# Latent attention in steps of four heads instead of two, in a four-layer mixer kernel on one core

## The chip, the cores and the metric

The kernel runs on one core of one Trainium2 chip. The metric is device time in microseconds of one execution of the whole program; lower is better. The core has TensorE (PE) for matrix products and transpositions, VectorE (DVE) and ScalarE (ACT) for element-wise work and reductions, GpSimd (POOL) and DMA queues. PE reads SBUF and writes only to PSUM, which the kernel uses as eight banks of 128 x 512 fp32. DVE and ACT take results out of PSUM.

## The reference

The program is four layers of `x = x + attention(norm(x)) * silu(ffn(norm(x)))` over 8192 tokens of width 128 (32 sequences of 256 tokens). Only the attention of layer 0 is touched by the change:

```python
# D_MODEL, N_HEADS, N_KV, HEAD_DIM, D_LAT = 128, 8, 2, 128, 32;  N_REP = 4
q = (x @ wq).reshape(Bq, Tq, N_KV, N_REP, HEAD_DIM)
k_lat = (x @ wk_down).reshape(Bq, Tq, N_KV, D_LAT)
v_lat = (x @ wv_down).reshape(Bq, Tq, N_KV, D_LAT)
k = jnp.einsum('bkhl,ld->bkhd', k_lat, wk_up)
v = jnp.einsum('bkhl,ld->bkhd', v_lat, wv_up)
scores = jnp.einsum('bqhrd,bkhd->bhrqk', q, k) * scale
scores = jnp.where(causal, scores, jnp.finfo(scores.dtype).min)
probs = jax.nn.softmax(scores, axis=-1)
y = jnp.einsum('bhrqk,bkhd->bqhrd', probs, v)
return y.reshape(Bq, Tq, N_HEADS * HEAD_DIM) @ wo
```

The up-projections are folded into `wq` and `wo` beforehand, so keys, queries and values have 32 elements per head, and four heads fill the 128 partitions.

## The kernel before

`first_layer` runs: the norm, the routing of tokens to experts, `latent_attention` for sequences 0 to 15, the expert FFN, `latent_attention` for sequences 16 to 31, and the gate. The later layers follow and are the same before and after. So the changed function runs twice (a run is called a half below), each time over `pairs` = 8 pairs of sequences (index `i`; `u` is the sequence of the pair). Each engine has its own program, written out in full; engines meet only through counting semaphores (`STEPS`), where `S["exps"].at(i, j)` is the value reached when step `j` of pair `i` is done. An engine runs its list in order, so a wait holds up everything behind it.

A sequence has 8 heads, in two groups `c` of four (one key/value head each). Before, a **step** `j` is two heads, four steps to a sequence. Of one step:

- PE, `pe_scores` (L699 to L706): for each of the two heads a 128 x 256 and a 128 x 128 block of scores (the causal blocks only) from 32 partitions, into one bank a head; then masks added by four 64 x 64 bf16 products (L706). Steps alternate between banks 0-1 and 2-3, so the scores of `j` wait for the exponentials of `j - 2`.
- DVE, `rowmax` (L876, L877): the negated row maxima, out of the two banks.
- ACT, `exps` (L838): four exponentials with row sums.
- PE, `pe_turn` (L715): six 128 x 128 transpositions of the probabilities into banks 4 and 5; DVE copies both banks at once to SBUF (L898, 128 x 768).

Every second step, `pe_mix` (L727) multiplies four heads' transposed probabilities with the values into bank 6. Once a sequence: key, query and value projections (L743, L743, L754), the spread of the inverse row sums (`pe_spread`, L737), the product of the two on DVE (`ot`, L891) and the output projection (L749), all through bank 7. ACT copies queries, spread sums, values and outputs (L854, L850, L861, L865), DVE copies keys (L902). POOL widens the inverse sums (L803), copies the input (L809), and issues four indirect DMAs a sequence (L518 scatter, L526 gather) that have to do with the experts.

The order of the work around the change is that of the bodies of `body(i)`: in turn `t`, PE does scores `t + 1`, transpositions `t - 1`, the value product every second turn, and one of the once-a-sequence products.

Of the kernel before, what the change touches and what calls it, by code (L numbers as in the profile page):

```python
# [27 lines left out]
P = 128  # L28
# [42 lines left out]
class Stage:  # L71
# [21 lines left out]
    "projected", "freed_act", "freed_dve", "scores", "masked", "rowmax", "exps", "turned", "turned_sb",  # L93
# [576 lines left out]
def latent_attention(nc, ps, m, w, first_pair, pairs, move, weights):  # L670
# [4 lines left out]
    with ExitStack() as mem:  # L675
# [5 lines left out]
        pr, nm, pt = buf("probs", P, 2, 2, W), buf("minus_max", P, 2, 2, 2), buf("probs_t", P, 4, 2, W)  # L681
# [7 lines left out]
        def pe_scores(pe, i, j):  # L689

            u, c, s = j % 8 // 4, j % 4 // 2, j % 2
            pe.wait_ge(*S["exps"].at(i, j - 2))
            if j % 4 == 0:
                pe.wait_ge(*S["k_sb"].at(i, j // 4))
                pe.wait_ge(*S["q_sb"].at(i, j // 4))
            b0 = 2 * s
            for e in range(2):
                rows = slice(32 * (2 * s + e), 32 * (2 * s + e) + 32)
                pe.matmul(ps[:, b0 + e, P:W], qt[rows, u, c, P:T], kt[rows, u, c, :], start=True, stop=False)  # L699
            for e in range(2):  # L700
                rows = slice(32 * (2 * s + e), 32 * (2 * s + e) + 32)
                pe.matmul(ps[:, b0 + e, 0:P], qt[rows, u, c, 0:P], kt[rows, u, c, 0:P], start=False, stop=False)
            for e in range(2):
                rows = slice(64 * e, 64 * e + 64)
                for h in range(2):
                    mm = pe.matmul(bank(ps, b0 + e, 3, P)[64 * h:64 * h + 64, ::2], one[rows, rows],  # L706
                                   hide[rows, h:h + 1].to_broadcast([64, 2, P]), start=False, stop=True)
            mm.then_inc(*S["scores"].inc)

        def pe_turn(pe, i, j):  # L710
            pe.wait_ge(*S["exps"].at(i, j))
            pe.wait_ge(*S["turned_sb"].at(i, j - 1))
            for e in range(2):
                for k in range(3):
                    mm = pe.transpose(ps[:, 4 + e, k * P:(k + 1) * P], pr[:, j % 2, e, k * P:(k + 1) * P], m["ident"][:])  # L715
            mm.then_inc(*S["turned"].inc)

        def pe_mix(pe, i, g):

            u, c = g % 4 // 2, g % 2  # L720
            pe.wait_ge(*S["turned_sb"].at(i, 2 * g + 1))
            pe.wait_ge(*S["v_sb"].at(i, g // 2))
            if c == 0:
                pe.wait_ge(*S["attended"].at(i, g // 2 - 1))
            for kb in range(2):
                for r in range(4):
                    mm = pe.matmul(ps[32 * r:32 * r + 32, 6, c * T + kb * P:(c + 1) * T], v[:, u, kb, c * LAT:(c + 1) * LAT],  # L727
                                   pt[:, (2 * g + r // 2) % 4, r % 2, kb * T:T + kb * P], start=(kb == 0), stop=(kb == 1))
            mm.then_inc(*S["mixed"].inc)

        def pe_spread(pe, i, n):
            pe.wait_ge(*S["widened"].at(i, n))
            if here(i, n + 2, 2):
                pe.wait_ge(*S["k_sb"].at(i, n + 2))
# [23 lines left out]
        names = dict(copied=2, scores=8, rowmax=8, exps=8, turned=8, turned_sb=8, mixed=4, rowsum=2, widened=2, spread=2,  # L758
                     spread_sb=2, attended=2, q_ps=2, q_sb=2, k_ps=2, k_sb=2, v_ps=2, v_sb=2, o_ps=2, o_sb=2)
        with Stage(pairs, **names), Stage(1, moved0=TOK), nc.Block() as block:  # L760
            @block.tensor
            def _(pe):
                def body(i):
                    for t in range(8):
                        u, at = t // 4, t % 4
                        if here(i, t + 1, 8):
                            pe_scores(pe, i, t + 1)
                        if here(i, t - 1, 8):
                            pe_turn(pe, i, t - 1)
                        if t % 2 and here(i, (t - 3) // 2, 4):  # L770
                            pe_mix(pe, i, (t - 3) // 2)
                        if at == 0 and here(i, u - 1, 2):
                            pe_spread(pe, i, u - 1)
                        if at == 1 and here(i, u + 1, 2):
                            pe.wait_ge(*S["k_sb"].at(i, u + 1))
                            pe.wait_ge(*S["spread_sb"].at(i, u - 1))
                            pe_project(pe, i, u + 1, lambda c: wq[:, c], "q_ps")
                        if at == 2:
                            if here(i, u + 1, 2):
                                pe.wait_ge(*S["q_sb"].at(i, u + 1))  # L780
                            if here(i, u - 1, 2):
                                pe_out(pe, i, u - 1)
                            if here(i, u + 1, 2):
                                pe_v(pe, i, u + 1)
                        if at == 3 and here(i, u + 2, 2):
                            pe.wait_ge(*S["o_sb"].at(i, u - 1))
                            pe.wait_ge(*S["v_sb"].at(i, u + 1))
                            pe.wait_ge(*S["copied"].at(i, u + 2))
                            pe_project(pe, i, u + 2, lambda c: wk[:, c].rearrange("p r l -> p (r l)"), "k_ps")

                written_out(pairs, 1, 1, body)
# [33 lines left out]
            def _(act):  # L825
                act.preload_act_table_set("exp_and_others")

                def exps(i, j):
                    u, c, s = j % 8 // 4, j % 4 // 2, j % 2
                    act.wait_ge(*S["rowmax"].at(i, j))  # L830
                    act.wait_ge(*S["turned"].at(i, j - 2))
                    if j % 4 == 0:
                        act.wait_ge(*S["rowsum"].at(i, j // 4 - 2))
                    for e in range(2):
                        head = 4 * c + 2 * s + e
                        for qb in range(2):
                            span = slice(qb * P, P + qb * T)
                            last = act.activation(pr[:, j % 2, e, span], ps[:, 2 * s + e, span], ACT.Exp,  # L838
                                                  bias=nm[:, s, qb, e:e + 1], accum_out=sums[:, u, qb, head:head + 1])
                    last.then_inc(*S["exps"].inc)  # L840

                def body(i):
                    for t in range(8):
                        u, at = t // 4, t % 4
                        if here(i, t, 8):
                            exps(i, t)
                        if at == 0 and here(i, u - 1, 2):
                            act.wait_ge(*S["spread"].at(i, u - 1))
                            act.wait_ge(*S["attended"].at(i, u - 2))
                            act.activation(rt[:], ps[:, 7], ACT.Copy).then_inc(*S["spread_sb"].inc)  # L850
                        if at == 1 and here(i, u + 1, 2):
                            act.wait_ge(*S["q_ps"].at(i, u + 1))
                            act.wait_ge(*S["scores"].at(i, 4 * u - 1))
                            act.activation(qt[:, 1 - u], bank(ps, 7, 2, T), ACT.Copy).then_inc(*S["q_sb"].inc)  # L854
                        if at == 2:
                            if here(i, u - 1, 2):
                                act.wait_ge(*S["o_ps"].at(i, u - 1))
                            if here(i, u + 1, 2):
                                act.wait_ge(*S["v_ps"].at(i, u + 1))
                                act.wait_ge(*S["mixed"].at(i, 2 * u - 1))  # L860
                                act.activation(v[:, 1 - u], ps[:, 7, T:T + P].rearrange("p (t l) -> p t l", t=2),  # L861
                                               ACT.Copy).then_inc(*S["v_sb"].inc)
                            if here(i, u - 1, 2):
                                act.wait_ge(S["first"].sem, PRIME)
                                act.activation(m["s"][:, bass.ds((i * 2 + 2 * first_pair + u - 1) * T, T)], ps[:, 7, 0:T], ACT.Copy)\  # L865
                                    .then_inc(*S["o_sb"].inc)

                written_out(pairs, 1, 1, body)

            @block.vector  # L870
            def _(dve):
                def rowmax(i, j):
                    s = j % 2
                    dve.wait_ge(*S["scores"].at(i, j))
                    dve.wait_ge(*S["exps"].at(i, j - 2))
# [1673 lines left out]
```

## Time and profile before

| | us |
|---|---|
| three runs: median (lowest, highest) | 2933.48 (2930.82, 2941.59) |
| the profiled execution: its own time | 2933.75 |
| span of its trace | 2932.0 |
| PE busy | 2690.3 (92%) |
| DVE busy | 2159.2 (74%) |
| ACT busy | 1948.2 (66%) |
| POOL busy | 1060.5 (36%) |
| mean granted clock of TensorE | 0.956 |

The span holds many stages with different limits, so shares over the span say little of this change. In a timeline row the first number is the start from the start of the span, the second the time from the first start to the last end of the merged instructions, then engine, line, operation, tiles and shapes; a bracket at the end gives the idle time before it and who ended it. A matmul on fp32 shows as two records, a transposition as one. Ends of matmuls are modelled, so the distance from one start to the next start of the same engine is the better measure of what a piece of work takes on PE; the second number is what the engines that wait for it see.

### The profile page before, as it was taken

To read this page: it belongs to the slowest core of one execution; us is meant where nothing else is said; L and a number is where in the kernel's file an instruction comes from. 1 tells how busy PE (TensorE), PEld (TensorE's weight loads), DVE (VectorE), ACT (ScalarE), POOL (GpSimd) and SP (SyncE) were. 2 spreads that over 40 slices of the span, in tenths; PEclk is the share of its full clock that TensorE was granted. 3 is DMA by queue.
4 is the path that set the end of the run, shared out by engine and by line. 5 is a ranking of instruction groups with operands and counts; after the bars stand their busy time and mean duration, and the time that the engine had idled before them with its cause. 6 is when DMAs were issued, how large, how long until landed. Compare 5 with 4: busy or idle time off the path is not lost. (4 is left out here: it accounts for less than half of the span.)

```text
span 2932.0 us, 62151 instructions
## 1 busy us (share of the span) xinstructions
PE 2690.3 (92%) x21644; PEld 1794.8 (61%) x21644; DVE 2159.2 (74%) x3742; ACT 1948.2 (66%) x5578; POOL 1060.5 (36%) x1228
## 2 busy tenths in 40 slices
PE   7799899997889879978879999999898999999898
PEld 4577797774554444445537777777444777777644
DVE  4576565776674569956769999998446999999766
ACT  4366565666763464435359999998446999999744
POOL 0233343331000254410035555564214655555431
PEclk9799998998999979979989999999998999999999
DMA  4200121000000000022000000000000000000000
GB/s 145 76 22 21 47 73 29 20 23 12 9 17 0 1 1 0 0 61 31 9 20 2 2 2 2 2 2 2 20 1 9 2 2 2 2 2 2 2 22 36
DMA packets 83170, 53.93 MB, mean 18 GB/s; under 512 B 28848, under 2 KB 75568, under 8 KB 82864
## 3 DMA queue, kind: packets, MB, share of 16 engines
q1 hardware_dynamic: 78768, 41.56, 5.1%
q0 software_dynamic: 4096, 8.40, 1.0%
q8 instruction: 179, 2.93, 0.4%
q14 instruction: 127, 1.04, 0.1%
HBM read 31.59 MB, written 18.35 MB: 17 GB/s over the span
## 5 line engine op out<-in xcount | busy, mean ns | idle before, releaser
L2149 ACT ACTIVATE probs<-banks,minus_max,rnorm 128x128 f32<-128x128 f32 x1024 | 460.0, 469 | 4.2 <-DVE minus_max L2245 2.8
L2021 PE MATMUL banks<-weights,hf 128*128 128x512 f32 x768 | 429.6, 643 | 24.5 <-POOL hf L462 13.5
L2064 POOL TENSOR_TENSOR qk_cross<-qk_raw,rope_scaled 128x512 f32<-128x512 f32 x256 | 325.5, 1272 | 25.4 <-ACT qk_raw L2182 11.5
L2074 POOL TENSOR_TENSOR qk_rot<-qk_rot,rnorm 128x512 f32<-128x512 f32 x128 | 133.5, 1043 | 291.3 <-DVE qk_rot L2278 282.9
L2149 ACT ACTIVATION_READ_ACCUMULATOR probs<-banks,minus_max,rnorm 128x1 f32 x1024 | 222.6, 217 | 0.0
L838 ACT ACTIVATE probs<-banks,minus_max 128x128 f32<-128x128 f32 (+1 forms) x512 | 207.9, 425 | 13.2 <-DVE minus_max L877 11.8
L2225 DVE COPY probs_t<-banks 128x512 f32<-128x512 f32 x256 | 175.8, 687 | 53.7 <-PE banks L1999 53.5
L1999 PEld LDWEIGHTS banks<-ident,probs 128*128 128x128 f32 x1024 | 126.9, 141 | 134.4 <-issue 134.4
L2271 DVE TENSOR_TENSOR qk_rot<-qk_raw,rope_scaled 128x512 f32<-128x512 f32 x256 | 175.5, 726 | 0.0
L2259 DVE TENSOR_REDUCE sumsq<-qk_sq 128x16 f32<-128x1024 f32 x128 | 154.8, 1209 | 26.9 <-issue 19.9
L2030 PE MATMUL banks<-ident,qk_rot 128*128 128x128 f32 x1024 | 159.7, 279 | 10.2 <-DVE qk_rot L2278 5.0
L2278 DVE TENSOR_TENSOR qk_rot<-qk_rot,qk_cross 128x1024 f32<-128x1024 f32 x128 | 161.5, 1261 | 4.4
L2241 DVE TENSOR_REDUCE minus_raw<-banks 128x8 f32<-128x1024 f32 x128 | 155.5, 1215 | 7.0 <-PE banks L1991 7.0
L1999 PE MATMUL banks<-ident,probs 128*128 128x128 f32 x1024 | 153.9, 273 | 6.0 <-DVE probs_t L2225 5.8
L2021 PEld LDWEIGHTS banks<-weights,hf 128*128 128x128 f32 x768 | 117.4, 192 | 53.0 <-POOL hf L462 15.1
L2013 PE MATMUL banks<-v_tok,probs_t 128*64 128x64 f32 x3072 | 148.4, 226 | 0.0
L2464 DVE SCALAR_TENSOR_TENSOR qk_rot<-banks,b1t,qk_rot 128x512 f32<-128x512 f32 x96 | 71.9, 750 | 103.3 <-ACT qk_rot L2417 89.1
L441 POOL TENSOR_SCALAR ln_rows<-ln_rows,ln_moments,ln_scale 128x128 f32<-128x128 f32 x64 | 49.8, 792 | 254.4 <-ACT ln_scale L423 254.4
L2030 PEld LDWEIGHTS banks<-ident,qk_rot 128*128 128x128 f32 x1024 | 114.7, 142 | 41.8 <-issue 38.6
L2013 PEld LDWEIGHTS banks<-v_tok,probs_t 128*64 128x64 f32 x3072 | 130.6, 138 | 11.9 <-issue 10.0
L2115 PE MATMUL banks<-ot,weights 128*128 128x128 f32 x1024 | 136.3, 276 | 0.0
L2163 ACT ACTIVATE qk_sq<-qk_raw 128x1024 f32<-128x1024 f32 x128 | 134.2, 1048 | 0.1
(356 smaller groups left out, 6976.2 us busy)
## 6 DMA issues: line engine op xcount, KB each, us to landing
sorted_x<-zero_rows SPq DMA_DIRECT2D x10, 512.0 KB
rows_in<-sorted_x SPq DMA_DIRECT2D x18, 256.0 KB, 3.1
sorted_y<-rows_out SPq DMA_DIRECT2D x18, 256.0 KB, 2.4
x_res<-in_x SPq DMA_DIRECT2D x8, 512.0 KB, 7.1
out_x<-x_res SPq DMA_DIRECT2D x16, 256.0 KB, 2.0
w1b<-in_L_ffn_w SPq DMA_DIRECT2D x8, 256.0 KB
s_branch<-in_L_ffn_w SPq DMA_DIRECT2D x8, 256.0 KB
w1g<-in_L_ffn_W SPq DMA_DIRECT2D x8, 256.0 KB, 3.0
```

Source lines behind the costliest of these rows:

```text
L838: last = act.activation(pr[:, j % 2, e, span], ps[:, 2 * s + e, span], ACT.Exp, bias=nm[:, s, qb, e:e + 1], accum_out=sums[:, u, qb, head: ...
L1999: mm = pe.transpose(ps[:, 4, n * P:(n + 1) * P], pr[:, k % 2, 4 * h + n], m["ident"][:])
L2013: mm = pe.matmul(ps[64 * w:64 * w + 64, 5, at], pt[:, h, n * P + 64 * w:n * P + 64 * w + 64], vm[:, at] if tb and not w else va[:, k % 4, ...
L2021: pe.matmul(ps[:, misc(k, j)], hf[:, n // 2 % 2, 0, n % 2 * P:(n % 2 + 1) * P], wqkv[:, w:w + QW], start=True, stop=True).then_inc(*S[name ...
L2030: mm = pe.transpose(ps[:, misc(k, j), c * P:(c + 1) * P], st[:, n % 4, first:first + P], m["ident"][:])
L2064: return pool.tensor_tensor(by_half(tw[:, n, at]), by_half(qk[:, n, at])[:, :, ::-1, :], tab[:, n, 2 * w + 1].rearrange("p (a d) -> p a d" ...
L2149: last = act.activation(pr[:, k % 2, head], ps[:, 2 * (k % 2) + par, c * P:(c + 1) * P], ACT.Exp, scale=rn[:, k % 4, head:head + 1], bias= ...
L2225: dve.tensor_copy(pt[:, h], ps[:, 4]).then_inc(*S["turned_sb"].inc)
L2241: dve.tensor_reduce(nr[:].rearrange("p (b c) -> p b c", b=2), ps[:, 2 * (k % 2):2 * (k % 2) + 2].rearrange("p b (c t) -> p b c t", c=4), A ...
L2259: dve.tensor_reduce(ss[:], by_head(sq[:]), AX.X, ALU.add).then_inc(*S["sumsq"].inc)
L2271: last = dve.tensor_tensor(by_head(st[:, n, at]), by_head(qk[:, n % 2, at]), tab[:, n % 2, 2 * w:2 * w + 1].to_broadcast([P, HEADS, DH]), ...
L2278: dve.tensor_tensor(st[:, n], st[:, n], tw[:, n % 2], ALU.add).then_inc(*S["rotated"].inc)
```

## The change

The unit of work becomes the group `g` of four heads, two to a sequence. `pe_scores` fills banks 0 to 3 at once, so there is no second set of banks, and the scores of `g` wait for the exponentials of `g - 1`. All eight mask products stand together; a signal is given after the fourth and after the eighth. The twelve transpositions of a group go in three lots of four, each to one whole bank, 4 or 5 in turn. They are those of the group before, `g - 1`. ACT copies the first lot (`lead_sb`), ahead of its exponentials of `g`, DVE the other two. The value products of `g - 2` stand ahead of the scores of `g`. The copies of keys and those of queries and of spread sums change engines: keys go from DVE to ACT, the other two from ACT to DVE. The key projection is one sequence ahead instead of two.

```diff
-        pr, nm, pt = buf("probs", P, 2, 2, W), buf("minus_max", P, 2, 2, 2), buf("probs_t", P, 4, 2, W)
+        pr, nm, pt = buf("probs", P, 2, 4, W), buf("minus_max", P, 2, 2, 2, 2), buf("probs_t", P, 2, 4, W)
-        def pe_scores(pe, i, j):
-            pe.wait_ge(*S["exps"].at(i, j - 2))
+        def pe_scores(pe, i, g):
+            u, c = g % 4 // 2, g % 2
+            pe.wait_ge(*S["exps"].at(i, g - 1))
+            if c == 0:
+                pe.wait_ge(*S["k_sb"].at(i, g // 2))
+                pe.wait_ge(*S["q_sb"].at(i, g // 2))
+            for r in range(4):
+                rows = slice(32 * r, 32 * r + 32)
+                pe.matmul(ps[:, r, P:W], qt[rows, u, c, P:T], kt[rows, u, c, :], start=True, stop=False)
+            for r in range(4):
+                rows = slice(32 * r, 32 * r + 32)
+                pe.matmul(ps[:, r, 0:P], qt[rows, u, c, 0:P], kt[rows, u, c, 0:P], start=False, stop=False)
+            for s in range(2):
+                for e in range(2):
+                    rows = slice(64 * e, 64 * e + 64)
+                    for h in range(2):
+                        mm = pe.matmul(bank(ps, 2 * s + e, 3, P)[64 * h:64 * h + 64, ::2], one[rows, rows],
+                                       hide[rows, h:h + 1].to_broadcast([64, 2, P]), start=False, stop=True)
+                mm.then_inc(*S["scores"].inc)
+        def pe_turn(pe, i, g, t):
+            if t == 0 and not here(i, g + 1, 4):
+                pe.wait_ge(*S["exps"].at(i, g))
+            if t == 2:
+                pe.wait_ge(*S["lead_sb"].at(i, g))
+            else:
+                pe.wait_ge(*S["turned_sb"].at(i, 2 * (g - 1) + t))
+            for k in range(4):
+                mm = pe.transpose(ps[:, 4 + (g + t) % 2, k * P:(k + 1) * P], blocks(pr, g, t)[:, k * P:(k + 1) * P],
+                                  m["ident"][:])
...
             @block.tensor
             def _(pe):
+                def slot(i, g):
+                    u = g // 2
+                    if here(i, g - 2, 4):
+                        pe_mix(pe, i, g - 2)
+                    if here(i, g, 4):
+                        pe_scores(pe, i, g)
+                    if here(i, g - 1, 4):
+                        pe_turn(pe, i, g - 1, 0)
+                    if g % 2 == 0 and here(i, u - 1, 2):
+                        pe_spread(pe, i, u - 1)
+                    if g % 2 == 1 and here(i, u + 1, 2):
+                        pe.wait_ge(*S["k_sb"].at(i, u + 1))
+                        pe_project(pe, i, u + 1, lambda c: wq[:, c], "q_ps")
+                    if here(i, g - 1, 4):
+                        pe_turn(pe, i, g - 1, 1)
+                        pe_turn(pe, i, g - 1, 2)
+                    if g % 2 == 0 and here(i, u + 1, 2):
...
+                            pe.wait_ge(*S["spread_sb"].at(i, u - 1))
...
+                        pe_project(pe, i, u + 1, lambda c: wk[:, c].rearrange("p r l -> p (r l)"), "k_ps")
+                    if g % 2 == 1:
...
+                            pe.wait_ge(*S["q_sb"].at(i, u + 1))
...
+                            pe_out(pe, i, u - 1)
...
+                            pe_v(pe, i, u + 1)
...
             def _(act):
+                def slot(i, g):
...
+                        act.activation(blocks(pt, g - 1, 0), ps[:, 4 + (g - 1) % 2], ACT.Copy).then_inc(*S["lead_sb"].inc)
+                    if here(i, g, 4):
+                        exps(i, g)
...
             def _(dve):
+                def turned(i, g, t):
+                    dve.wait_ge(*S["turned"].at(i, 3 * g + t))
+                    if t == 1:
+                        dve.wait_ge(*S["mixed"].at(i, g - 2))
+                    dve.tensor_copy(blocks(pt, g, t), ps[:, 4 + (g + t) % 2]).then_inc(*S["turned_sb"].inc)
```

On PE, two of the four steps of a sequence in the steady part before: scores (`kt,qt`), masks (`hide`), six transpositions (`ident,probs`), with the once-a-sequence products between.

```order
244 L699 MATMUL banks<-kt,qt 128x256 x2
245 L702 MATMUL banks<-kt,qt 128x128 x2
246 L706 MATMUL banks<-hide,ident_bf 64x2x128 x4
247 L715 MATMUL banks<-ident,probs 128x128 x6
248 L749 MATMUL banks<-ot,wo_lat 128x256 x2
249 L754 MATMUL banks<-wvd,xf 128x64 x2
250 L699 MATMUL banks<-kt,qt 128x256 x2
251 L702 MATMUL banks<-kt,qt 128x128 x2
252 L706 MATMUL banks<-hide,ident_bf 64x2x128 x4
253 L715 MATMUL banks<-ident,probs 128x128 x6
```

The same engine and place of the changed kernel: one slot (the odd one of a sequence), then the value products that stand ahead of the next scores.

```order
232 L701 MATMUL banks<-kt,qt 128x256 x4
233 L704 MATMUL banks<-kt,qt 128x128 x4
234 L709 MATMUL banks<-hide,ident_bf 64x2x128 x8
235 L721 MATMUL banks<-ident,probs 128x128 x4
236 L752 MATMUL banks<-xf,wq_lat 128x256 x2
237 L721 MATMUL banks<-ident,probs 128x128 x8
238 L758 MATMUL banks<-ot,wo_lat 128x256 x2
239 L763 MATMUL banks<-wvd,xf 128x64 x2
240 L735 MATMUL banks<-probs_t,v_tok 32x256 x4
241 L735 MATMUL banks<-probs_t,v_tok 32x128 x4
```

Four heads' scores and masks now stand in one block instead of two, and only once-a-group work follows until the next block. The count of products and transpositions is as before.

DVE in the steady part, before: maxima and copies of 768 columns alternate, with `kt` and `ot` between.

```order
148 L886 RECIPROCAL inv_sums<-row_sums 128x16
149 L876 TENSOR_REDUCE minus_max<-banks 128x2
150 L877 TENSOR_REDUCE minus_max<-banks 128x2
151 L898 COPY probs_t<-banks 128x768
152 L876 TENSOR_REDUCE minus_max<-banks 128x2
153 L877 TENSOR_REDUCE minus_max<-banks 128x2
154 L898 COPY probs_t<-banks 128x768
155 L891 TENSOR_TENSOR ot<-banks,inv_spread 128x512
```

The same of the changed kernel, one sequence: even slot, then odd slot.

```order
146 L901 RECIPROCAL inv_sums<-row_sums 128x16
147 L886 TENSOR_REDUCE minus_max<-banks 128x2 x4
148 L914 COPY inv_spread<-banks 128x512
149 L894 COPY probs_t<-banks 128x512 x2
150 L906 TENSOR_TENSOR ot<-banks,inv_spread 128x512
151 L886 TENSOR_REDUCE minus_max<-banks 128x2 x4
152 L917 COPY qt<-banks 128x512
153 L894 COPY probs_t<-banks 128x512 x2
```

The copies of the transposed probabilities now come after the copy of spread sums or queries, which come after all four maxima.

## Rows read from the trace of the kernel before

**Rows 1.** The table of windows: window and length, busy us of each engine, clock, DMA.
```profile
95.72:317.81 222.09, 216.23 (x1984) 158.66 (x1984) 145.84 (x240) 133.57 (x577) 77.23 (x96) 0.96 0.14 42
239.56:252.51 12.95, 12.95 (x126) 9.61 (x126) 9.08 (x16) 8.23 (x36) 4.80 (x7) 1.00 0.07 22
102.91:115.26 12.35, 12.35 (x59) 8.65 (x58) 4.72 (x8) 4.95 (x22) 3.94 (x5) 0.50 0.91 242
440.00:467.00 27.00, 23.12 (x202) 22.50 (x200) 12.98 (x28) 14.74 (x23) 9.24 (x22) 1.00 0.18 50
1010.00:1050.00 40.00, 25.33 (x132) 22.51 (x132) 31.09 (x200) 34.48 (x108) 35.31 (x46) 0.74 0.00 1
```

**Rows 2.** The timeline of PE over one sequence of the steady part.
```profile
243.22 0.70 PE L699 MATMUL banks<-kt,qt 32*128 32x256 f32 x4
...
244.07 0.30 PE L706 MATMUL banks<-hide,ident_bf 64*64 64x256 bf16 x4
244.30 0.87 PE L715 MATMUL banks<-ident,probs 128*128 128x128 f32 x6
245.01 1.03 PE L749 MATMUL banks<-ot,wo_lat 128*128 128x256 f32 x4
245.88 0.55 PE L754 MATMUL banks<-wvd,xf 128*128 128x64 f32 x4
246.36 0.70 PE L699 MATMUL banks<-kt,qt 32*128 32x256 f32 x4
...
248.26 0.86 PE L727 MATMUL banks<-probs_t,v_tok 128*32 128x256 f32 x16
249.04 1.13 PE L743 MATMUL banks<-xf,wk_lat 128*128 128x256 f32 x4
250.10 0.70 PE L699 MATMUL banks<-kt,qt 32*128 32x256 f32 x4
...
251.90 0.60 PE L737 MATMUL banks<-ident,inv_wide 128*128 128x128 f32 x4
252.43 0.70 PE L699 MATMUL banks<-kt,qt 32*128 32x256 f32 x4
```

**Rows 3.** The timeline of ACT, same sequence.
```profile
246.96 0.37 ACT L838 ACTIVATE probs<-banks,minus_max 128x128 f32<-128x128 f32 x1
...
247.75 0.38 ACT L838 ACTIVATE probs<-banks,minus_max 128x128 f32<-128x128 f32 x1
...
248.45 0.23 ACT L838 ACTIVATION_READ_ACCUMULATOR probs<-banks,minus_max 128x1 f32 x1
...
252.54 0.60 ACT L850 ACTIVATE inv_spread<-banks 128x512 f32<-128x512 f32 x1 [2.19 <-PE banks L737]
253.03 0.36 ACT L838 ACTIVATE probs<-banks,minus_max 128x128 f32<-128x128 f32 x1
```

**Rows 4.** The timeline of DVE, same sequence.
```profile
243.58 0.69 DVE L891 TENSOR_TENSOR ot<-banks,inv_spread 128x512 f32<-128x512 f32 x1 [1.00 <-PE banks L727]
244.43 0.42 DVE L876 TENSOR_REDUCE minus_max<-banks 128x2 f32<-128x256 f32 x1 [0.16 <-PE banks L706]
244.77 0.68 DVE L877 TENSOR_REDUCE minus_max<-banks 128x2 f32<-128x512 f32 x1
245.37 0.95 DVE L898 COPY probs_t<-banks 128x768 f32<-128x768 f32 x1
...
250.21 0.69 DVE L902 COPY kt<-banks 128x512 f32<-128x512 f32 x1 [0.76 <-PE banks L743]
250.82 0.24 DVE L886 RECIPROCAL inv_sums<-row_sums 128x16 f32<-128x16 f32 x1
```

**Rows 5.** More of the timelines of PE and POOL, one mix earlier.
```profile
241.37 0.86 PE L727 MATMUL banks<-probs_t,v_tok 128*32 128x256 f32 x16
241.82 0.96 POOL L518 DMA_INDIRECT sorted_x<-token_rows,row_of_token  x1 [0.30 <-issue]
```

**Rows 6.** Who waited for whom, 130 to 320 us: total, times, longest.
```profile
DVE ot L891 <- PE banks L727: 13.7, 14, 1.0
```

More of the change, by code:

```diff
@@ L710, in pe_turn, with blocks @@
[L710 to L715, printed above, removed]
+        def blocks(x, g, t):
+            return x[:, g % 2].rearrange("p h w -> p (h w)")[:, 4 * t * P:4 * (t + 1) * P]
+        def pe_scores(pe, i, g):
[17 more added lines that the diff above has]
+                mm.then_inc(*S["scores"].inc)
@@ L793, in _ @@
+                written_out(pairs, 1, 1, lambda i: [slot(i, g) for g in range(4)])
             @block.gpsimd
@@ L826, in _ @@
                 act.preload_act_table_set("exp_and_others")
[L828 to L839, printed above, removed]
-                    last.then_inc(*S["exps"].inc)
@@ L842, in body @@
[L842 to L866, printed above, removed]
@@ L868, in _, with exps @@
-                written_out(pairs, 1, 1, body)
+                def exps(i, g):
+                    u, c = g % 4 // 2, g % 2
+                    act.wait_ge(*S["turned"].at(i, 3 * (g - 2) + 2))
+                    if c == 0:
+                        act.wait_ge(*S["rowsum"].at(i, g // 2 - 2))
+                    for s in range(2):
+                        act.wait_ge(*S["rowmax"].at(i, 2 * g + s))
+                        for e in range(2):
+                            for qb in range(2):
+                                span = slice(qb * P, P + qb * T)
+                                head = 4 * c + 2 * s + e
+                                last = act.activation(pr[:, g % 2, 2 * s + e, span], ps[:, 2 * s + e, span], ACT.Exp,
+                                                      bias=nm[:, g % 2, s, qb, e:e + 1],
+                                                      accum_out=sums[:, u, qb, head:head + 1])
+                    last.then_inc(*S["exps"].inc)
@@ L870, in _ @@
+                written_out(pairs, 1, 1, lambda i: [slot(i, g) for g in range(4)])
             @block.vector
             def _(dve):
[L872 to L875, printed above, removed]
-                    dve.tensor_reduce(nm[:, s, 0], ps[:, 2 * s:2 * s + 2, 0:P], AX.X, ALU.max, negate=True)
-                    dve.tensor_reduce(nm[:, s, 1], ps[:, 2 * s:2 * s + 2, P:W], AX.X, ALU.max, negate=True)\
-                        .then_inc(*S["rowmax"].inc)
@@ L904, in _, with rowmax @@
-                written_out(pairs, 1, 1, body)
+                def rowmax(i, g, s):
+                    dve.wait_ge(*S["scores"].at(i, 2 * g + s))
+                    dve.wait_ge(*S["exps"].at(i, g - 2))
+                    for qb in range(2):
+                        last = dve.tensor_reduce(nm[:, g % 2, s, qb], ps[:, 2 * s:2 * s + 2, qb * P:P + qb * T], AX.X,
+                                                 ALU.max, negate=True)
+                    last.then_inc(*S["rowmax"].inc)
+                def turned(i, g, t):
[3 more added lines that the diff above has]
+                    dve.tensor_copy(blocks(pt, g, t), ps[:, 4 + (g + t) % 2]).then_inc(*S["turned_sb"].inc)
@@ L905, in latent_attention @@
+                written_out(pairs, 1, 1, lambda i: [slot(i, g) for g in range(4)])
         S["loaded"].base += 16 * len(weights)
```

130 lines of the change are left out of this document (57 added, 73 removed).

## The prediction

> **What bounds the kernel now.** I read the windows first, then the timelines of PE, ACT and DVE over one sequence, then the list of waits.
>
> The window table shows the first half from the first input copy to the last output copy: 222.09 us for 16 sequences. In its steady part one sequence takes 12.95 us, and PE is busy for all 12.95 of them, at a granted clock of 1.00, that is 2.4 GHz. DVE is busy 9.08 us and ACT 8.23 us [rows 1]. So PE sets the pace. The second half is the same code with another DMA. 16 x 12.95 = 207.2 us; the other 15 us of a half are the start, where PE stood at half clock (0.50, 1.2 GHz) for 12.35 us [rows 1], and the run-out.
>
> What PE does with a step is in its timeline, read from start to start. Scores of two heads take 244.07 - 243.22 = 0.85 us, masks 0.23, six transpositions 0.71 (0.12 each), output 0.87, values 0.48, mix 0.78, keys 1.06, spread 0.53 [rows 2]. Most of these are full-array work that the change keeps. The scores are not: a step uses two of the four 32-row bands of the array.
>
> **What the change takes away on PE.** Scores for four heads in one block: two blocks of 0.85 become one. The trace has no four row bands at once. The nearest row is the mix, four 32-column bands at once: four products of 256 columns and four of 128 in 0.78 us, with changes of shape around them [rows 2]. The lower bound is that four bands cost what two do, 0.85 + 0.02; the upper bound that they go two and two, 0.85 + 0.65 (the second pair's columns alone: 0.43 for 256, half of the output's 0.87, and 0.22 for 128). I take 0.87, as the mix row shows four bands together. Masks: 0.23 for four, of which 0.11 is columns; eight take 0.34. So a group's block takes 1.21 instead of 2 x 1.08 = 2.16; 0.95 saved a group, 1.9 a sequence. PE's work falls to about 11.05 us a sequence.
>
> The Trainium skill, page "TensorE: Matmul & The Clock Gate", Part 3, states a measured 3.07 times for four 32-row tiles of 512 columns, not 4. No run here shows it yet. By it the 256-column part would take about 0.43 x 4 / 3.07 = 0.56 us instead of 0.43, and my total would come out 8 us higher, as an estimate.
>
> **What it adds: a ring.** Scores now fill all four banks, so the scores of g wait for the last exponential of g - 1, which waits for maxima, which wait for scores. Walk one slot, time 0 at the first product of the scores:
>
> - DVE sees the first signal at 1.22 (243.22 to 244.43 before [rows 2, 4]). Maxima take 0.34 and 0.60 per two heads [rows 4]; the first pair's are there at 1.22 + 0.34 + 0.68 = 2.24, DVE is free at 3.10.
> - PE ends scores and masks at 1.21, the first lot of transpositions at 1.68. ACT sees it at about 1.9 and copies it; such a copy of 128 x 512 holds ACT 0.49 (252.54 to 253.03 [rows 3]). The exponentials start at 2.40, not 2.24: here the added copy is on the path, for 0.16.
> - A head's two exponentials take 0.79 (246.96 to 247.75), the last record ends 0.14 after that (248.45 + 0.23 against 246.96 + 1.58) [rows 3]. Four heads: 3.30. They end at 5.70. With 0.05 for the signal the next scores could start at 5.75: **the ring alone gives 11.5 us a sequence.**
>
> PE and DVE must fit under it. In the **even** slot PE adds spread (to 2.21) and two lots (to 3.15), then waits for DVE's copy of the spread sums before it may write the keys into bank 7. DVE comes to that copy only after the four maxima, at 3.10, and it ends at 3.79 (0.69 as `kt` [rows 4]). Keys 3.85 to 4.85. The mix of the group waits for DVE's second lot: copies hold DVE 0.61 each (250.21 to 250.82 [rows 4]), so 3.71, 4.32, end 5.01. Mix 5.06 to 5.84. In the **odd** slot PE does queries (0.86 without changes of shape) to 2.54, lots to 3.48, waits for the query copy (DVE again 3.10 to 3.79), then output to 4.82, values to 5.30, mix to 6.08. DVE has its lots done at 5.01, ACT its exponentials at 5.70. ACT's work in a sequence is 2 x (0.49 + 3.30) + keys 0.49 + values and output about 0.45 = 8.5, DVE's about 8.3: neither is full.
>
> So a sequence takes 5.84 + 6.08 = 11.92 us. Of the 1.9 saved on PE 1.03 reach the clock on the wall. PE now waits 1.28 us a sequence for DVE copies that stand behind the maxima (0.70 for the spread sums, 0.21 before the mix, 0.37 for the queries), and gets 0.4 of that back as changes of shape that fall into the waits.
>
> **The moved waits.** Keys one sequence ahead instead of two: their copy on ACT is wanted by the query product at 1.68 of the odd slot, and is done 0.5 after the last exponential, before 0.6; free. `ot` stands ahead of the maxima in the odd slot: with the mix's end at 0.08 it runs 0.1 to 0.8, in DVE's idle time before 1.22; free. The widening on POOL (0.6) and its input to the spread are wanted at 1.68 and start at 0.2; free. POOL's four DMA issues have 5 us of work in 11.9; free.
>
> **Start and run-out.** The last group has no neighbour to hide in. After the last exponential there are three lots (1.4) and one copy of 0.69 before the mix, against 0.85 and 0.95 before: + 0.4 with signals. The last exponentials stand alone for 3.3 us instead of 1.7: + 1.6. At the start PE runs at half clock and the first transpositions come one group later: + 1. I take 3 us a half, bounds 0 and 6.
>
> **Sum.** 32 sequences x 1.03 = 33 us, less 2 x 3 = 27 us. The profiled execution took 2933.75 (span 2932.0, 1.75 around it), 0.3 above the median of the runs. 2933.5 - 27 = **2906 us**, 0.9% less. What a measurement of this kernel can tell from no change is about 0.5%, 15 us either way.
>
> **Rivals.**
>
> *The ring decides (2893 us).* PE's waits come out shorter than walked, as DVE may pass earlier. Then 2 x 5.75 = 11.5, 1.45 x 32 - 6 = 40 us gained. For it: all its terms are pitches read on ACT. Against: DVE's order puts the spread and query copies behind all maxima. 12%.
>
> *A late signal of the mix (2925 us).* Once a sequence the mix ended at 241.37 + 0.86 = 242.23, but DVE, idle for 1.00, began `ot` only at 243.58: 1.35 late, 14 times in a row [rows 4 to 6]. It coincides with the third DMA issue on POOL, 241.82 [rows 5]. Before, nobody on the path waits for it. Now `ot` stands ahead of the maxima; 1.35 late it ends at 2.04 and the ring turns 0.6 later, once a sequence: + 19 us. Against: POOL's issues move in phase, from about 1.4 of the even slot on, and the mix is elsewhere. 9%.
>
> *Half of it lost in signals (2918 to 2932).* PE now restarts from a semaphore three or four times a sequence where it never waited; 0.15 more each than my 0.05 is 32 x 0.5 = 16 us. 8%.
>
> *The bands do not overlap four at a time (2949 us, slower).* Place: the scores block. If pairs go one after the other, each of 64 groups costs 0.65 more, and it is on the ring, where nothing hides it: 42 - 27 = 15 us slower, 2949 from 2933.5. It decides from a block of 1.21 + 27 / 64 = 1.63 us on. For it: only two row bands are ever seen at once here. Against: four column bands and four quadrants (masks) run together [rows 2]. 10%.
>
> *The clock (2915 to 3010).* PE, never idle now, will idle about 1.3 us in 11.9. In a stage where PE was busy 25.33 of 40 us the granted clock was 0.74 on average; with 23.12 of 27 us it was 1.00 [rows 1]. The changed stage has about nine tenths, so I expect 1.00. If it fell as in the first of these, PE work of 10.7 us would at times double and the gain would be gone several times over. 4%.
>
> **How the numbers follow.** The forecast has 57%, with its own range of 2896 to 2917 (0.15 us either way in each slot or 3 us a half). Faster by over 0.5% (below 2919): 57 + 12 + 3 from the lower ends of the three middle cases = 72%. Slower by over 0.5% (above 2948): two thirds of the bands' case, whose own spread is 2940 to 2958, and three quarters of the clock's, 10%. Within: 18%. For 8 in 10 the range takes the forecast's, most of the ring's and the two partial cases: 2889 to 2932.
>
> **What would show it.** In the changed profile: one sequence of the steady part takes 11.9 us, PE about 90% busy at 1.00. From the first scores to the first transposition 1.2 us; 1.8 would mean that bands went two by two. The exponentials of a group start about 2.4 after its scores and come out of ACT's copy, not out of the maxima. PE's waits name DVE's copy of `inv_spread` and `qt`, about 0.7 and 0.4. If PE's longest wait is for `probs` on ACT instead, the ring decides. If DVE's `ot` waits for the mix again, the late signal came along. A sequence above 12.5 us, or a clock under 1.00 in mid-half, makes the forecast wrong.

## The result and the profile after

Changed kernel: 2941.85 us, median of 12 runs (2932.22 to 2949.39). Kernel before, on the same chips: 2935.78 us, 12 runs (2930.82 to 2942.21). The ratio is 1.002, 95% interval 1.001 to 1.003: 0.2% slower. The interval leaves out 1, and the difference is inside the 0.5% that the forecast counts as no change. The forecast was 2906 us with a range of 2889 to 2932; the time lies above both. The profiled execution has a span of 2937.5 us (before 2932.0).

The page of the changed kernel, its span and the busy times of the engines:

```profile
span 2937.5 us, 61992 instructions
PE 2634.6 (90%) x21644; PEld 1755.4 (60%) x21644; DVE 2143.9 (73%) x3774; ACT 1958.1 (67%) x5610; POOL 1060.0 (36%) x1228
```

The window table of the changed kernel over the first half, cut at the first and the fourteenth `ot` (start, steady part of 13 sequences, run-out), and one steady sequence. The columns are those of [rows 1].

```profile
93.80:123.40 29.60, 22.56 (x164) 15.82 (x165) 10.67 (x20) 14.25 (x56) 9.10 (x12) 0.66 0.62 176
123.40:293.40 170.00, 143.89 (x1616) 109.14 (x1619) 111.15 (x208) 111.19 (x481) 62.07 (x77) 0.99 0.07 22
293.40:322.50 29.10, 21.04 (x212) 15.13 (x212) 15.52 (x28) 13.13 (x56) 6.03 (x7) 0.88 0.04 12
253.84:266.90 13.06, 10.91 (x128) 8.30 (x128) 8.53 (x16) 8.55 (x37) 4.80 (x6) 1.00 0.07 21
```

PE's work in a sequence did fall as forecast, from 12.95 [rows 1] to 10.91 us, at a granted clock of 1.00. But the sequence takes 13.06 us: the saved 2 us came back as idle time. Cut in the same way, the kernel before took 31.3, 168.1 and 23.8 us. So the first half is 1.7 shorter at the start, 1.9 longer in the steady part and 5.3 longer in the run-out; the second half 4.4 shorter, 2.0 longer and 5.3 longer. Together attention lost 8.4 us; the rest of the program is 2.9 us shorter by the two traces.

Where PE stands idle is seen in its timeline, an odd slot (from 253.71) and an even slot (from 259.78). Columns as in [rows 2]; the bracket is idle time and what ended it.

```profile
253.71 0.71 PE L701 MATMUL banks<-kt,qt 32*128 32x256 f32 x8
254.25 0.40 PE L704 MATMUL banks<-kt,qt 32*128 32x128 f32 x8
254.58 0.41 PE L709 MATMUL banks<-hide,ident_bf 64*64 64x256 bf16 x8
254.92 0.66 PE L721 MATMUL banks<-ident,probs 128*128 128x128 f32 x4
...
257.54 1.13 PE L758 MATMUL banks<-ot,wo_lat 128*128 128x256 f32 x4 [0.22 <-DVE qt L917]
...
259.78 0.71 PE L701 MATMUL banks<-kt,qt 32*128 32x256 f32 x8
...
261.92 1.07 PE L721 MATMUL banks<-ident,probs 128*128 128x128 f32 x8
263.70 1.10 PE L752 MATMUL banks<-xf,wk_lat 128*128 128x256 f32 x4 [0.71 <-issue]
266.01 0.86 PE L735 MATMUL banks<-probs_t,v_tok 128*32 128x256 f32 x16 [1.22 <-DVE probs_t L894]
266.80 0.71 PE L701 MATMUL banks<-kt,qt 32*128 32x256 f32 x8
```

The block of scores and masks takes 254.92 - 253.71 = 1.21 us, the odd slot 259.78 - 253.71 = 6.07 (walked: 1.21 and 6.08). The even slot takes 266.80 - 259.78 = 7.02 instead of 5.84. Its mix starts 6.23 after the scores, not 5.06, and waits 1.22 us for a copy on DVE. DVE over the same even slot:

```profile
261.00 1.95 DVE L886 TENSOR_REDUCE minus_max<-banks 128x2 f32<-128x256 f32 x4 [1.29 <-PE banks L709]
262.87 0.68 DVE L914 COPY inv_spread<-banks 128x512 f32<-128x512 f32 x1
263.47 0.68 DVE L894 COPY probs_t<-banks 128x512 f32<-128x512 f32 x1
265.18 0.69 DVE L894 COPY probs_t<-banks 128x512 f32<-128x512 f32 x1 [1.03 <-remote]
266.93 0.69 DVE L906 TENSOR_TENSOR ot<-banks,inv_spread 128x512 f32<-128x512 f32 x1 [1.06 <-PE banks L735]
```

The last copy reads the third lot of transpositions. PE had ended it at 261.92 + 1.07 = 262.99, and DVE's walk has the copy at 4.32 of the slot. It begins at 5.40, idle for 1.03 before and with no producer that the profile can name ("remote"). PE's signal came 2.19 us late. POOL at that time issues indirect DMAs:

```profile
260.88 0.98 POOL L518 DMA_INDIRECT sorted_x<-token_rows,row_of_token  x1 [0.15 <-issue]
262.17 0.95 POOL L518 DMA_INDIRECT sorted_x<-token_rows,row_of_token  x1 [0.30 <-issue]
263.43 0.96 POOL L518 DMA_INDIRECT sorted_x<-token_rows,row_of_token  x1 [0.30 <-issue]
```

That it is the signal that is late, and not its reader, is seen in the times of the semaphore updates that the packed trace keeps (not all are recorded). The update for the third lot stands at 265.15, 2.16 after the end of its transpositions. Three more of PE's updates are late in this slot: masks by 0.37, spread by 0.14, keys by 0.41. From 130 to 280 us every recorded update of DVE, ACT and POOL follows the end of its instruction by 0.01, in this kernel and in the one before.

The list of waits, 130 to 310 us (total, times, longest), says how often:

```profile
PE banks L735 <- DVE probs_t L894: 17.0, 13, 3.2
DVE ot L906 <- PE banks L735: 15.8, 14, 1.7
DVE probs_t L894 <- remote: 10.4, 11, 1.1
PE banks L758 <- DVE qt L917: 2.6, 12, 0.2
```

Once a sequence the mix waits for that copy. `ot`, which had the late signal before ([rows 6], 13.7 us), still waits about as long in total, but the 1.06 before the row at 266.93 is nearly all the mix's own 0.86 and no late signal: `ot` begins 0.06 after the mix's end (266.01 + 0.86).

The run-out repeats the pattern at a worse place: there all four issues stand close together (300.11, 301.39, 302.66, 303.92). PE's first lot of transpositions and ACT's copy of it, then PE at the last mix but two:

```profile
300.55 0.66 PE L721 MATMUL banks<-ident,probs 128*128 128x128 f32 x4
302.21 0.60 ACT L874 ACTIVATE probs_t<-banks 128x512 f32<-128x512 f32 x1 [2.78 <-PE banks L721]
```

```profile
306.72 1.51 PE L735 MATMUL banks<-probs_t,v_tok 128*32 128x256 f32 x16 [3.21 <-DVE probs_t L894]
308.16 1.24 PE L701 MATMUL banks<-kt,qt 32*128 32x256 f32 x8
```

The lot ends at 300.55 + 0.66 = 301.21 and ACT, idle, starts its copy 1.00 later; so ACT, too, gets PE's signal late, and here the exponentials behind it start 3.36 after their scores (302.70 - 299.34) instead of 2.39. After 3.21 us of idling the same eight products (16 records) take 1.51 instead of 0.86 us: the granted clock fell to its lower level (1.2 GHz) for some 7 us, which is the 0.88 of the run-out window.

### The profile page after: what moved, and what is told of

Its sections match the earlier page's. It is cut to its first block and busy times, and to the rows that moved or that the text cites. A ratio compares the mean times of both kernels' runs of the same rounds, so it can differ in the third digit from the quotient of the medians.

```text
span 2937.5 us, 61992 instructions
## 1 busy us (share of the span) xinstructions
PE 2634.6 (90%) x21644; PEld 1755.4 (60%) x21644; DVE 2143.9 (73%) x3774; ACT 1958.1 (67%) x5610; POOL 1060.0 (36%) x1228
## 5 line engine op out<-in xcount | busy, mean ns | idle before, releaser
L886 DVE TENSOR_REDUCE minus_max<-banks 128x2 f32<-128x256 f32 (+1 forms) x256 | 124.9, 550 | 72.8 <-PE banks L709 72.8
L2259 DVE TENSOR_REDUCE minus_raw<-banks 128x8 f32<-128x1024 f32 x128 | 155.5, 1215 | 7.3 <-PE banks L2009 7.3
L874 ACT ACTIVATE probs_t<-banks 128x512 f32<-128x512 f32 x64 | 38.2, 597 | 152.4 <-PE banks L721 152.4
L2031 PEld LDWEIGHTS banks<-v_tok,probs_t 128*64 128x64 f32 x3072 | 130.7, 138 | 11.9 <-issue 10.0
```

The source lines that it names most:

```text
L2031: mm = pe.matmul(ps[64 * w:64 * w + 64, 5, at], pt[:, h, n * P + 64 * w:n * P + 64 * w + 64], vm[:, at] if tb and not w else va[:, k % 4, ...
L2259: dve.tensor_reduce(nr[:].rearrange("p (b c) -> p b c", b=2), ps[:, 2 * (k % 2):2 * (k % 2) + 2].rearrange("p b (c t) -> p b c t", c=4), A ...
```

## The experiments

Theory A, formed on these traces: GpSimd's indirect DMAs, issued in close succession, hold back PE's signals, and this hold, not the walk, makes the sequence 13.1. Rivals: TensorE's own queue makes the signals late in the new order (B), or the clock does (C); the added waits between PE, DVE and ACT cost more than walked; and, if the DMAs matter, it is their traffic and not the issue. "Sequence" below is the distance between two `ot`. All edits but the second and fourth are on the changed kernel. The loop that they replace issues three DMAs at once and a fourth behind the query copy; it stands under `if here(i, u, 2):` and is

```
for t in itertools.islice(tiles, TOK // (2 * pairs) - 1):
    move(pool, t)
if here(i, u + 1, 2):
    pool.wait_ge(*S["q_sb"].at(i, u + 1))
move(pool, next(tiles))
```

**1. The DMAs of a half after its loop (changed kernel).**

```
 # in place of the five lines: nothing; behind the loop over i and u:
+for t in tiles:
+    move(pool, t)
```

> The changed kernel with the 64 indirect DMAs of each half issued by GpSimd after the attention loop instead of four a sequence within it; nothing else differs. Read are the distance from one ot to the next (13.1 us in 10 of 13 steady sequences of the changed kernel, 12.37 once) and whether VectorE still waits for the second lot of transpositions in the even slot (1.03 us). The total rises by 2 x 64 x 1.27 = about 160 us of issues laid end to end, and says nothing. Theory A (while GpSimd issues indirect DMAs close together, TensorE's completion signals reach the other engines 1 to 2 us late, and in the new ring somebody on the path is always waiting for one): the sequence falls to 11.9 to 12.1 us, the value that the forecast walked, and the wait for the second lot vanishes. The run-out (29.1 us from the last but two ot to the end) gets 2 to 3 us shorter. Rival B (the late signals come from TensorE itself, for instance from its queue of loads and waits, in the new order): the sequence stays at 13.1. Rival C (the power or clock state): stays at 13.1 too, with the granted clock under 1.00.

3063.14 us in one run, since 64 DMAs now stand alone behind each half. Every steady sequence takes 11.96 us. No copy waits for "remote", and from 130 to 280 us no recorded update of PE is over 0.04 late. The two last sequences, from the fourteenth `ot` to the sixteenth, take 22.2 us instead of 26.5; 4.3 shorter, where I had expected 2 to 3. B is out, since PE's program is unchanged; C is out, since the sequence of 13.06 us ran at a clock of 1.00 as well. Its even slot on PE:

```profile
239.50 1.10 PE L752 MATMUL banks<-xf,wk_lat 128*128 128x256 f32 x4 [0.70 <-DVE inv_spread L910]
240.70 0.86 PE L735 MATMUL banks<-probs_t,v_tok 128*32 128x256 f32 x16
```

The keys still wait 0.70 us for the copy of the spread sums, as walked; the mix starts 0.10 after the end of the keys and waits for no named engine. The walk was right to 0.04 us a sequence, and what it left out is the DMAs.

**2. The same in the kernel before.**

```
 # the same edit in before
+for t in tiles:
+    move(pool, t)
```

> The kernel before, with the same edit: the indirect DMAs after the loop. Theory A: the sequence stays at 12.95 us, since TensorE is busy throughout and nobody on its path waits for the late signal; but ot follows the mix by about 0.05 instead of 1.35 us. Rival B: ot stays 1.35 us late. If the sequence falls below 12.9, the DMAs cost the kernel before something as well, and part of what theory A gives to the new ring was there before.

3091.16 us in one run; the sequence stays at 12.95. The hold was there before and cost nothing. DVE of this run, around the same mix as in [rows 4, 5], which ended at 239.81:

```profile
239.20 0.95 DVE L894 COPY probs_t<-banks 128x768 f32<-128x768 f32 x1
240.07 0.68 DVE L887 TENSOR_TENSOR ot<-banks,inv_spread 128x512 f32<-128x512 f32 x1
```

`ot` starts 0.26 after the mix's end, right behind DVE's copy; with the DMAs it was 1.35.

**3. The four DMAs of a sequence apart.**

```
+for after in (None, S["rowmax"].at(i, 4 * u + 1), S["exps"].at(i, 2 * u), S["rowmax"].at(i, 4 * u + 3)):
+    if after:
+        pool.wait_ge(*after)
+    move(pool, next(tiles))
```

> The changed kernel with the four indirect DMAs of a sequence spaced out: the first after the copy of the input as now, the second once the maxima of the even slot are done, the third after its exponentials, the fourth once the maxima of the odd slot are done. Issues are then 1.8 to 3.3 us apart instead of 1.27; output and amount of work are the same. Theory A with closeness as the condition (before, the first and second issue and the lone fourth delayed nothing, the third did): sequence 11.9 to 12.2 us, and the whole kernel 20 to 25 us under the changed one, about 2918, so faster than the kernel before by 0.5 to 0.8%. Theory A' (every issue delays signals for some time, wherever it stands): the sequence stays at 12.8 to 13.3, the whole within 5 us of the changed kernel. Rival B: no difference.

2909.31 us (2908.24 to 2911.64, 4 runs), 0.9908 of before, interval 0.9885 to 0.9932. The sequence is 12.21. Same DMAs, same count, 2.4 to 3.7 us apart. The sequence is at the upper end of what theory A gave, the total 9 us below it. What is left shows in one row of DVE, odd slot, beside POOL's issue:

```profile
244.52 0.96 POOL L518 DMA_INDIRECT sorted_x<-token_rows,row_of_token  x1 [1.60 <-ACT probs L850]
```

```profile
245.88 1.95 DVE L885 TENSOR_REDUCE minus_max<-banks 128x2 f32<-128x256 f32 x4 [0.65 <-PE banks L709]
```

The maxima of the odd slot begin 0.25 late (0.65 of waiting, 0.40 where no issue is near), and they stand on the ring. So even a single issue costs, if it falls beside work whose signal someone waits for.

**4. The DMAs apart in the kernel before.**

```
+for k in range(4):
+    if k:
+        pool.wait_ge(*S["exps"].at(i, 4 * u + k - 1))
+    move(pool, next(tiles))
```

> The kernel before with the four indirect DMAs spaced out by its steps (each of the last three after one step's exponentials, 3.2 us apart). Theory A with closeness: sequence 12.95 as before, ot follows the mix at once. Theory A': ot or another reader of a TensorE signal is late somewhere, still without effect on the 12.95. Rival B: ot 1.35 us late as before.

2933.61 us in one run, sequence 12.95. This experiment failed in part: the first two events that I waited for had passed or nearly so. Three issues stayed 1.3 to 1.5 us apart (241.13, 242.42, 243.92), and the hold came along:

```profile
245.43 0.69 DVE L890 TENSOR_TENSOR ot<-banks,inv_spread 128x512 f32<-128x512 f32 x1 [1.01 <-PE banks L727]
```

The mix had ended at 243.22 + 0.86 = 244.08, 1.35 earlier. It agrees with run 2 that the old kernel does not care, and says nothing on spacing there.

**5. Two and two.**

```
+for after in (None, None, S["rowmax"].at(i, 4 * u + 3), None):
+    if after:
+        pool.wait_ge(*after)
+    move(pool, next(tiles))
```

> The changed kernel with two indirect DMAs back to back in the even slot, where three stand now, and two back to back in the odd slot, after its maxima. Theory A with the third close issue as the condition (the hold of TensorE's signals always ended 2.99 us after the start of the second issue of three close ones, never with one alone): sequence 11.96 to 12.2 us. Theory A with any two close issues as the condition: both slots are hit or one is, 12.4 to 13.1 us. Rival B (place in the ring alone, not closeness): between 12.2 and 12.6, by which signal falls near an issue.

2904.47 us in one run (before on this chip: 2932.2). Sequences of 11.96 and 12.24 mostly alternate in the steady part of the first half, with one of 12.84 at its end; they are 12.0 to 12.7 in the second. That is neither the one version of theory A (up to 12.2) nor the other (from 12.4). Pairs 1.3 us apart still hold signals, but mostly at a point with slack:

```profile
252.70 1.29 DVE L893 COPY probs_t<-banks 128x512 f32<-128x512 f32 x2 [0.18 <-PE banks L721]
```

The second lot ended at 250.89 + 0.60 = 251.49 and its copy starts 1.2 later, but DVE had other work for most of that and idled 0.18; the mix then waited 0.36. So two close issues are not harmless either. That their place decides what they cost fits this row and is not tested by itself.

**6. Apart, and away from the scores' signal.**

```
+for after in (None, S["rowmax"].at(i, 4 * u + 1), S["rowmax"].at(i, 4 * u + 2), S["turned_sb"].at(i, 4 * u + 1)):
+    if after:
+        pool.wait_ge(*after)
+    move(pool, next(tiles))
```

> As the spaced-out version (12.21 us a sequence), but with the third and fourth issue moved within the odd slot: the third after the maxima of the first two heads, the fourth after the second lot's copy of the odd slot. In the spaced-out version the third issue came 1.1 us before the signal of the odd slot's scores, which was then 0.25 us late. Theory A: that wait goes, sequence 11.96 us as with no DMA in the loop, total 8 us under the spaced-out version, about 2901, ratio to the kernel before 0.988. Rival: another signal takes the same hold (output, values or mix, all with room), or the 0.25 us were the cost of any issue near the ring: 12.1 to 12.3, 2908.

2902.36 us (2899.13 to 2904.81, 4 runs), against 2932.2 (7 runs): 0.9892, interval 0.9876 to 0.9909. The sequence is 11.96, as expected. This version beats both kernels. Its windows, cut as above, save that the fourteenth `ot` is at 277.35, 0.25 before the cut:

```profile
94.00:121.90 27.90, 22.40 (x164) 15.82 (x168) 10.61 (x21) 14.10 (x56) 8.14 (x11) 0.64 0.64 185
121.90:277.60 155.70, 142.46 (x1616) 108.20 (x1618) 109.82 (x209) 111.28 (x482) 62.23 (x77) 1.00 0.07 24
277.60:302.60 25.00, 18.84 (x212) 13.71 (x212) 14.85 (x28) 13.48 (x57) 7.01 (x8) 1.00 0.05 16
```

and PE from an even slot's scores through the odd one:

```profile
235.44 0.71 PE L701 MATMUL banks<-kt,qt 32*128 32x256 f32 x8
...
239.36 1.10 PE L752 MATMUL banks<-xf,wk_lat 128*128 128x256 f32 x4 [0.70 <-DVE inv_spread L913]
240.55 0.86 PE L735 MATMUL banks<-probs_t,v_tok 128*32 128x256 f32 x16
241.34 0.71 PE L701 MATMUL banks<-kt,qt 32*128 32x256 f32 x8
...
245.16 1.13 PE L758 MATMUL banks<-ot,wo_lat 128*128 128x256 f32 x4 [0.22 <-DVE qt L916]
...
247.41 0.71 PE L701 MATMUL banks<-kt,qt 32*128 32x256 f32 x8
```

Even slot 5.90, odd slot 6.07 (walked 5.84 and 6.08). PE's busy time in the steady part is nearly that of the changed kernel (142.46 and 143.89), and to the fourteenth `ot` the part is 170.0 - 155.5 = 14.5 us shorter, the start 1.7 and the run-out 3.9, where the clock now stays at 1.00. The hold is not gone: behind a single issue (234.62, the next at 236.71) the trace has PE's update for the mix 0.45 late (end 235.51, update 235.96), and nobody waits for it.

**7. The same transfers from the hardware queue.** SyncE issues plain DMAs of the same tiles, at about the same points (`pool` in these lines is the engine passed in; the gathers of the other half are changed alike); this leaves out the permutation of the rows.

```
-pool.indirect_dma_start(sorted_x[:], bass.IndirectOffsetOnAxis(r["pos"][:, t:t + 1], 0), rows[:, t], None)
+pool.dma_start(sorted_x[t * P:(t + 1) * P], rows[:, t])
```

> The changed kernel with the indirect DMAs replaced by plain ones of the same 64 KB, issued by SyncE on the hardware queue at the same points of the sequence (three close together after the copy of the input, one after the query copy). It leaves out the permutation: rows go to and come from their own place. Theory A1 (what holds TensorE's signals is GpSimd's software issue): sequence 11.96 to 12.1 us. Theory A2 (it is the transfers, or the burst of completion signals that each sends): sequence 12.4 to 13.1 us as in the changed kernel.

2903.05 us in one run; 11.96 in every steady sequence of both halves, and no "remote" in its waits:

```profile
PE banks L752 <- DVE inv_spread L921: 9.2, 13, 0.7
PEld banks L735 <- issue: 6.0, 13, 0.5
```

The bytes are there and the hold is not: no recorded update of PE from 130 to 280 us is over 0.04 late. That separates GpSimd's indirect DMAs from a transfer of the same bytes. It does not separate the issue from the scattered addresses, nor from the packets, which went with it: from 250 to 264 us this run moves 0.45 MB in 980 packets, the changed kernel 0.39 MB in 190.

**8. The first lot's copy on DVE (on top of 6).** This tests the ring: is it this copy on ACT that the exponentials wait for, and would they be earlier without it?

```
-act.activation(blocks(pt, g - 1, 0), ps[:, 4 + (g - 1) % 2], ACT.Copy).then_inc(*S["lead_sb"].inc)
+dve.tensor_copy(blocks(pt, g - 1, 0), ps[:, 4 + (g - 1) % 2]).then_inc(*S["lead_sb"].inc)   # behind both rowmax
```

> As the run with the placed DMAs, with the first lot of transpositions copied by VectorE behind the maxima instead of by ScalarE ahead of its exponentials. It tests the step of the walk that VectorE's work behind the maxima, not ScalarE's ring, sets both slots. If so, 0.61 us more on VectorE is added to each slot whole: even 5.84 to 6.45, odd 6.08 to 6.69, sequence 13.1 us, although the ring of scores, maxima and exponentials itself gets 0.12 us shorter (exponentials start 2.28 instead of 2.40 after the scores). Rival: the ring on ScalarE sets the slots: sequence 11.7 to 12.0.

2933.2 us in one run, sequence 13.15 (expected 13.1). The exponentials do come out of the maxima now and not out of ACT's copy, but only 0.04 earlier, 236.01 - 233.66 = 2.35 after their scores instead of 2.39 (expected 2.28). The copy stands behind four maxima, and PE's third lot waits for the bank that it frees:

```profile
237.48 0.66 PE L721 MATMUL banks<-ident,probs 128*128 128x128 f32 x4 [1.09 <-DVE probs_t L909]
```

```profile
PE banks L721 <- DVE probs_t L909: 20.9, 24, 1.1
```

The copy belongs on ACT. DVE's queue after the maxima is the tight place of this schedule, and what the copy costs the exponentials on ACT (0.16 walked, 0.04 by this run) is cheap.

## Why the prediction was wrong, point by point

- **PE's work.** Right. 10.91 us a sequence against 11.05 forecast; the block of scores and masks 1.21 against 1.21.
- **The bands.** Right, and the slower rival is false. Four 32-row bands take 254.58 - 253.71 = 0.87 us for 256 and 128 columns, two took 0.85 [rows 2]. The Trainium skill, page "TensorE: Matmul & The Clock Gate", Part 3, gives a measured speedup of 3.07 for four tiles of 32 rows and 512 columns. The 0.13 us that I had estimated from it for the 256-column part does not show in the trace: the whole block took 0.02 more than with two bands. No run here has 512 columns.
- **The walk of the two slots.** Right where nothing else interferes: 11.96 against 11.92 in runs 1, 6 and 7, with the waits where the walk has them (0.70 for the spread sums). The exponentials start at 2.39 (262.17 - 259.78) against 2.40. The wait for the query copy is 0.22 against 0.37. Of the walked 0.21 before the mix 0.09 lie between the keys' end (239.36 + 1.10) and the mix (240.55 in run 6). So PE idles about 1.0 where I had 1.28.
- **"POOL's four DMA issues have 5 us of work in 11.9; free."** This is the step that failed. I counted POOL's time and not what the issues do to others. Measured: the third lot's signal 2.19 us late, 1.1 of it past the slack, in nearly every sequence. By run 6 against the changed kernel it is 14.5 us of a half's steady part, 3.9 of the run-out and 1.7 of the start; over both halves 39 us in the lengths of attention (456.9 and 417.7). I had forecast a gain of 27; with the hold off the path it is about 30 (2932.2 - 2902.4), and the hold took more than all of it.
- **The rival of the late signal.** The mechanism was named, with its row, but placed on the mix and `ot` in the odd slot, for 19 us. It struck the third lot in the even slot, for twice that. My argument against it, that POOL's issues move in phase and the mix is elsewhere, was true and beside the point: with issues 1.3 us apart from 1.1 of the slot on, the question was which signal of PE falls in the next 3 us, not whether the mix does. One chain of waits along all PE signals from 1.1 to 5 of the even slot would have found the lot that ends at 3.21 and is wanted at 4.32.
- **Start and run-out.** I had + 3 us a half, + 1 for the start and + 2 for the run-out. In the first half of run 6 they are 27.9 - 31.3 = - 3.4 and 25.2 - 23.8 = + 1.4. But these stretches also hold three sequences beside the thirteen, one and two, each 0.99 shorter, which the forecast had counted apart. Without that gain the start is - 2.4, the run-out + 3.4, together + 1.0 against + 3. In the second half the start is 6.5 shorter and the run-out 2.5 longer; the same count gives - 5.5 and + 4.5, so - 1.0. The run-out was put too low, and the start had the wrong sign: I had not counted that PE, at half clock there, has less to do (22.40 us of work before the first `ot` against 29.25; argued, not tested). In the changed kernel the run-out is 5.3 longer than before.
- **The ring decides.** Not reached: exponentials end 5.7 after the scores, PE's next scores come at 5.90 and 6.07. Run 8 turned the other way.
- **The clock.** Right for the steady part (0.99 and 0.98 in the two halves). It fell for short stretches, worst behind the 3.21 us wait in the run-out. In runs 1, 6 and 7 it stays at 1.00 from the first `ot` of a half to its last, save for 3.4 us in the second run-out of run 6; so most of it came with the hold.
- **The chances.** A time within 0.5% of before had 18%. The cases that reach there were a late signal, lost signals and bands, each with its own size, and I let the first stand at 19 us at most, though its row (1.35 us, 14 times) bounds it only for the signal that it happened to hit.

What stays open: what in GpSimd's issue holds PE's signals, and what sets the length. Of three close issues the held signal mostly came 3.0 us after the second one's start (262.17 to 265.18, 301.39 to 304.40 in the run-out, 242.42 to 245.43 in run 4). With issues over 2 us apart the largest delay of a reader in the rows read was 0.25, and an update that nobody waited for was 0.45 late (run 6). No run changes the distance of the issues alone and their place alone, so what each is worth is open. Why one steady sequence in each half takes only 12.37 us (in the first the one before `ot` at 253.84) was not tested. Its three issues stand as elsewhere, but the update of the third lot comes 1.45 late instead of 2.16, 2.26 after the second issue.

## What to carry to other kernels

When a change turns a schedule bound by one engine into one bound by a ring of signals, delays that were free become the path: look in the trace of before for readers that start later than their producer's end, however harmless there, and ask which signals will fall beside the same cause after the change. Here GpSimd's indirect DMAs should stand more than 2 us apart and away from signals that someone waits for; a walk of the ring that left them out was right to 0.04 us a sequence once they were out of the way, and with them in it a sequence took a tenth longer than the walk (13.1 against 11.9).

## What was not expected of the hardware

- Indirect DMAs issued by GpSimd 1.3 us apart delay the arrival of TensorE's signals at VectorE by 1.35 us (before and run 4) to 2.19 us (changed kernel), and at ScalarE by 1.00 us (its run-out). VectorE's signal to TensorE for the keys was not held: 0.15 us from the copy's end beside the issues (262.87 + 0.68 to 263.70) as in run 6 (238.53 + 0.68 to 239.36), and every recorded update of DVE, ACT and POOL from 130 to 280 us comes 0.01 after its instruction. Plain DMAs of the same size from SyncE do not do it.
- A single issue beside a block of scores (244.52 to 245.48) still made its signal 0.25 us late (run 3), one before the end of a mix made its update 0.45 late (run 6).
- Four 32-row bands of 256 columns run in the time of two (0.87 and 0.85 us with the 128-column part).
